# Choosing two of three experts from token 0's own logits, with new orders for the attention stage

## What is computed

```python
x = x + matmul(fake_quant(layernorm(x)), fake_quant(ctx))          # (2,512,1024) @ (2,1024,1024)
h = layernorm(x)
ratio = mean|h[:, 153:]| / (mean|h[:, :153]| + 1e-8)               # one number per batch
logits = concat([h, ratio]) @ gate_w + gate_b                      # 3 logits per token
scores = softmax(logits); top_val, top_idx = top_k(scores, 2)
top_val = top_val / (sum(top_val) + 1e-8)
for i in range(2):
    e = top_idx[:, 0, i]                                           # token 0 chooses for the batch
    x = x + top_val[..., i:i+1] * (act_e(h @ w1[e] + b1[e]) @ w2[e] + b2[e])
```

## Time and profile before

| | us |
|---|---|
| median of 3 runs (406.9, 407.07, 407.93) | 407.07 |
| the profiled execution, whole time | 406.77 |
| its span, first to last instruction | 405.0 |
| TensorE busy | 389.3 |
| VectorE busy | 329.0 |
| ScalarE busy | 196.2 |
| GpSimd busy | 57.9 |

### The profile page before, as it was taken

One profiled execution on the slowest core, in us unless ns is written; L12 is line 12 of the kernel. 1 busy time (PEld: TensorE's weight loads), 2 busy tenths in 40 slices (PEclk: granted clock), 3 DMA queues, 4 the chain that ended last, 5 costly groups with the idle time before them and its releaser, 6 DMA issues.

```text
span 405.0 us, 5336 instructions
## 1 busy us (share of the span) xinstructions
PE 389.3 (96%) x1932; PEld 307.2 (76%) x1932; DVE 329.0 (81%) x512; ACT 196.2 (48%) x254; POOL 57.9 (14%) x78
## 2 busy tenths in 40 slices
PE   2998989999999999999999999999999999999996
PEld 1445736888878888888888888888888888888885
DVE  8699877187999987898799996496998965949983
ACT  3578554174337633671826355342476333425720
POOL 8748400000000002572100004000000000000000
PEclk9999999999999999999999999999999999999999
DMA  8992039523003788000000399600045770000112
GB/s 316 413 407 112 2 108 376 193 84 124 2 0 106 258 252 259 9 0 2 0 0 2 107 368 387 229 2 0 2 146 217 246 256 18 2 0 1 54 52 104
DMA packets 23326, 52.82 MB, mean 130 GB/s; under 512 B 1761, under 2 KB 1793, under 8 KB 23297
## 3 DMA queue, kind: packets, MB, share of 16 engines
q1 hardware_dynamic: 22592, 50.34, 35.0%
q0 software_dynamic: 640, 2.10, 1.5%
q10 hardware_dynamic: 64, 0.02, 0.0%
HBM read 48.26 MB, written 4.19 MB: 130 GB/s over the span
## 4 chain that ended last, share of the span: by engine, by line
PE 94%; DVE 2%; DMA 1%; ACT 1%; issue 1%; ACTq 1%; DVEq 0%
PE ps L1579 43%; PE ps L1551 38%; PE ps L1345 7%; PE ps L1391 2%; PE ps L1377 2%; DMA b1n<-in_L_ffn_b_dram 1%; PE ps L1354 1%; PE ps L1277 1%; ACT q1T L569 1%; PE ps L1412 1%; DVE xres L859 0%; ACTq L666 0%; PE ps L1333 0%; PE ps L1318 0%; ACT hT_hi L593 0%
## 5 line engine op out<-in xcount | busy, mean ns | idle before, releaser
L634 ACT ACTIVATE w_hi<-raw 128x1024 fp32r<-128x1024 f32 x88 | 88.5, 1053 | 45.5 <-DVE raw L985 23.9
L954 DVE TENSOR_TENSOR w_lo<-raw,w_hi 128x1024 fp32r<-128x1024 f32 x88 | 103.4, 1219 | 1.7 <-ACT w_hi L634 1.2
L1579 PE MATMUL ps<-hT_hi,w_hi 128*128 128x512 f32 x256 | 100.0, 390 | 0.0
L1579 PE MATMUL ps<-hT_lo,w_hi 128*128 128x512 f32 x256 | 99.7, 389 | 0.0
L1579 PE MATMUL ps<-hT_hi,w_lo 128*128 128x512 f32 x256 | 99.7, 389 | 0.0
L1551 PE MATMUL ps<-w_hi,a_hi 128*128 128x512 f32 x224 | 87.7, 392 | 0.7 <-DVE a_lo L1027 0.7
L1551 PE MATMUL ps<-w_hi,a_lo 128*128 128x512 f32 x224 | 87.2, 390 | 0.0
L1551 PE MATMUL ps<-w_lo,a_hi 128*128 128x512 f32 x224 | 87.2, 389 | 0.0
L722 ACT ACTIVATE act_f<-ps,b1T 128x512 f32<-128x512 f32 x32 | 22.1, 689 | 104.0 <-PE ps L1579 104.0
L1579 PEld LDWEIGHTS ps<-hT_hi,w_hi 128*128 128x128 f32 x256 | 48.1, 188 | 10.1 <-issue 0.2
L1579 PEld LDWEIGHTS ps<-hT_hi,w_lo 128*128 128x128 f32 x256 | 48.1, 188 | 10.1
(11 more groups left out here) (153 smaller groups left out, 376.2 us busy)
## 6 DMA issues: line engine op xcount, KB each, us to landing
raw<-in_L_ffn_w_dram SPq DMA_DIRECT2D x64, 512.0 KB, 5.5
raw<-in_ctx_dram SPq DMA_DIRECT2D x16, 512.0 KB, 11.5
xres<-in_x_dram SPq DMA_DIRECT2D x8, 512.0 KB, 9.6
b2row<-in_L_ffn_b_dram SPq DMA_DIRECT2D x4, 512.0 KB, 6.6
out_dram<-xres POOLq DMA_DIRECT2D x8, 256.0 KB, 8.0
out_dram<-xres SPq DMA_DIRECT2D x8, 256.0 KB, 2.0
small<-in_L_xattn_x_scale_dram ACTq DMA_DIRECT2D x2, 0.0 KB
small<-in_L_xattn_x_zp_dram ACTq DMA_DIRECT2D x2, 0.0 KB
```

Of the source, the lines that this page charges most:

```text
L634: nc.scalar.activation(w_hi[n % SLOTS][:, 2 * c:2 * c + 2, :], region(q)[:, 2 * c:2 * c + 2, :], ACT.Copy).then_inc(w_hi_ready, 1)
L954: V.tensor_tensor(w_lo[n % SLOTS][:, 2 * c:2 * c + 2, :], region(n % QUARTERS)[:, 2 * c:2 * c + 2, :], w_hi[n % SLOTS][:, 2 * c:2 * c + 2, ...
L1579: last = T.matmul(ps[:, G1_BANK + f % 2, :], w[q % SLOTS][:, k % TT, fs], h[:, k, :], start=n == 0, stop=n == 3 * KT - 1)
```

## The change

**Choosing.** `token_logits(b)` is new: 16 products whose stationary operand is the single column of token 0 of hT_hi or hT_lo and whose moving operand is the 8 columns of gate weights. They give token 0's logits in one partition, before the logits of the other tokens exist. `token_scores` reads them; `choose_experts` adds the router bias and compares the biased logits rather than the exponentials, so it needs neither `gate_turn` nor `gate_exp`. The maximum and minimum over all tokens that it used to leave for `gate_values` move into `gate_values`. `router_bias` is split in two (`ratio_sums`).

**b1.** Its transpose joins `turn_gate_weights` at the start; `turn_bias` on PE and `load_bias` on ACT go; DVE copies it in `gate_weights`.

**Memory and banks.** lgT of batch 0 gets a place of its own; b2row still holds batch 1's, so SP waits for batch 1's `gate_turn` ahead of b2row of pair 2. Q1T_BANK[5] is 4 (was 3), RATIO_BANK[0] is 5 (was 1).

**Orders.** SP loads context tiles 0 and 1 ahead of x tiles 2 and 3. The four tables change, and the lists of all engines with them. Batch 1's `add_terms` 0 to 2 now follow group f = 0 of the first expert, and its last token tile follows f = 1. In pair 0 the `bias_add` calls move from f = 4 to 7 to f = 0 to 3.

```diff
-CTX_ORDER = {"act": [5, 8, 10, 11, 15, 14],
-             "dve": [2, 4],
-             "pool": [0, 1, 3, 6, 7, 9, 12, 13]}
+CTX_ORDER = {"act": [0, 3, 4, 6, 8, 10, 11, 15],
+             "dve": [2],
+             "pool": [1, 5, 7, 9, 12, 13, 14]}
...
+            load_ctx(0)
+            load_ctx(1)
             load_x(2)
             load_x(3)
-            load_ctx(0)
-            load_ctx(1)
...
+                if p == TOP_K:
+                    sp.wait_ge(logit_ps, B)
                 sp.dma_start(b2row[:], b2[bass.ds(e, 1), :].to_broadcast([P, D])).then_inc(b2_in, 16)
...
+            def token_scores(b):
+
+                dve.wait_ge(token_ps, b + 1)
+                V.tensor_copy(token[:, 0:8], ps[0:1, LOGIT_BANK, 0:8]).then_inc(token_read, 1)
+                dve.wait_ge(token_read, b + 1)
+                then(V.tensor_tensor(token[:, 8:8 + NE], token[:, 0:NE], token[:, 4:4 + NE], ALU.add))
...
             def choose_experts(b):
 
-                dve.wait_ge(exp_ready, b + 1)
...
+                dve.wait_ge(token_read, b + 1)
+                then(V.tensor_tensor(token[:, 12:12 + NE], token[:, 8:8 + NE], gbias[0:1, :], ALU.add))
...
             def gate_values(b):
 
                 top, _, mid, a, c, d, e, f = (sel[:, i, :] for i in range(8))
+                dve.wait_ge(exp_ready, b + 1)
+                V.tensor_tensor(a, ex[:, 0, :], ex[:, 1, :], ALU.max)
+                then(V.tensor_tensor(c, ex[:, 0, :], ex[:, 1, :], ALU.min))
+                then(V.tensor_tensor(top, a, ex[:, 2, :], ALU.max))
...
+            def token_logits(b):
+
+                if b:
+                    pe.wait_ge(act_ready, TOP_K * KT)
+                else:
+                    pe.wait_ge(gw_ready, 1)
+                    pe.wait_ge(x1_ready, 3)
+                pe.wait_ge(hT_lo_ready, 2 * b * TT + 2)
+                n = 0
+                for k in range(KT):
+                    for h in (hT_hi, hT_lo):
+                        last = T.matmul(ps[0:1, LOGIT_BANK, 0:8], h[:, k, 0:1], gw_parts[:, k, :],
+                                        start=n == 0, stop=n == 2 * KT - 1)
+                        n += 1
+                last.then_inc(token_ps, 1)
...
-                    if p == 0 and f >= TT:
-                        bias_add(p, k)
-                    if p > 0 and f < TT:
+                    if f < TT:
                         bias_add(p, f)
...
                 if p == 1:
+                    token_scores(1)
                     h_lo(1, 2)
                 t1_sum(p)
+                if p == 1:
+                    ratio_sums(1)
+                    router_bias(1)
+                    choose_experts(1)
                 result(p, 1)
```

More of the change, by code:

```diff
@@ L133, in build @@
         b2row = sb("b2row", [P, D], F32)
-        lgT = b2row[0:8, 0:S]
         ctxq = [sb(f"ctxq{b}", [P, KT, D], F16, act_at + b * (KT * D * 2 + 2 * D * 4)) for b in range(B)]
@@ L153, in build @@
         ident_b = sb("ident_b", [P, P], F16, o); o += P * 2
+        gwn = sb("gwn", [KT, P * NE], F32, o)
+        lgT = [sb("lgT", [8, S], F32, o)[:], b2row[0:8, 0:S]]; o += S * 4
         assert o <= at_weights_end
@@ L595, in split_h @@
                                          ACT.Copy).then_inc(hT_hi_ready, 1)
-            def load_bias():
-                act.wait_ge(b1T_ps, 1)
-                nc.scalar.activation(b1T[:], ps[:, B1T_BANK, 0:NE * KT], ACT.Copy).then_inc(b1T_ready, 1)
             def gate_logits(b):
@@ L606, in gate_logits @@
                     act.wait_ge(logit_ps, b)
-                nc.scalar.activation(lgT, ps[0:8, LOGIT_BANK, :], ACT.Copy).then_inc(logitT_ready, 1)
+                nc.scalar.activation(lgT[b], ps[0:8, LOGIT_BANK, :], ACT.Copy).then_inc(logitT_ready, 1)
             def gate_exp(b):
@@ L909, in choose_experts @@
             def choose_experts(b):
[L911 to L923 removed]
+                dve.wait_ge(token_read, b + 1)
+                then(V.tensor_tensor(token[:, 12:12 + NE], token[:, 8:8 + NE], gbias[0:1, :], ALU.add))
+                score = lambda e: token[0:1, 12 + e:13 + e]
+                one = lambda i: pick[0:1, i:i + 1]
+                large, small_, top, low = (token[0:1, i:i + 1] for i in range(4))
+                V.tensor_tensor(large, score(0), score(1), ALU.max)
+                then(V.tensor_tensor(small_, score(0), score(1), ALU.min))
+                V.tensor_tensor(top, large, score(2), ALU.max)
+                then(V.tensor_tensor(low, small_, score(2), ALU.min))
+                V.tensor_tensor(one(0), score(0), top, ALU.is_lt)
+                V.tensor_tensor(one(1), score(1), top, ALU.is_lt)
+                V.tensor_tensor(one(2), score(1), low, ALU.is_le)
+                then(V.tensor_tensor(one(3), score(2), low, ALU.is_le))
                 V.scalar_tensor_tensor(out=expert[0:1, 2 * b:2 * b + 1], in0=one(1), scalar=1.0, in1=one(0),
@@ L1120, in _ @@
             ctx_constants()
+            x_offset()
             q1_scales(0, 1)
             q1_scales(1, 1)
-            x_offset()
-            term_constants()
             x_stats(2)
+            x_stats(3)
+            load_q1T(1)
             quant_ctx(2)
-            x_stats(3)
-            quant_ctx(4)
-            gate_weights()
             q1_scales(2, 2)
             quant_x(2)
-            load_q1T(3)
+            quant_x(3)
+            term_constants()
+            gate_weights()
             x_stats(4)
             x_stats(5)
+            split_row_term(0)
             split_col_term(0)
-            split_row_term(0)
             q1_scales(4, 2)
@@ L1142, in _ @@
             h_stats(1)
+            h_stats(2)
+            h_lo(0, 0)
             attn_add(0, 3)
-            h_lo(0, 0)
-            h_stats(2)
+            token_scores(0)
             h_stats(3)
@@ L1149, in _ @@
             x_stats(7)
+            tokens_abs(0)
             h_lo(0, 2)
+            ratio_sums(0)
+            router_bias(0)
             q1_scales(6, 2)
-            quant_x(7)
-            tokens_abs(0)
+            choose_experts(0)
             h_lo(0, 3)
             load_q1T(6)
-            router_bias(0)
+            load_q1T(7)
             choose_scores(0)
-            choose_experts(0)
-            gate_values(0)
+            w_lo_chunk(0, 0)
             split_row_term(1)
             split_col_term(1)
-            attn_add(1, 0)
-            attn_add(1, 1)
-            w_lo_chunk(0, 0)
+            gate_values(0)
             w_lo_chunk(0, 1)
@@ L1167, in _ @@
             w_lo_chunk(1, 1)
-            attn_add(1, 2)
+            attn_add(1, 0)
+            attn_add(1, 1)
             for p in range(PAIRS):
@@ L1186, in _ @@
                         else:
-                            pass
+                            attn_add(1, 2)
                     elif f == 1:
@@ L1244, in _ @@
                     choose_scores(1)
-                    choose_experts(1)
                 result(p, 4)
@@ L1409, in gate_turn @@
                 pe.wait_ge(logitT_ready, b + 1)
[L1410 removed]
+                if b:
+                    pe.wait_ge(ratio_read, b + 1)
+                else:
+                    pe.wait_ge(hT_lo_ready, 2 * TT)
                 for t in range(TT):
[L1412 removed]
+                    last = T.matmul(ps[:, TURN_BANK[b], 4 * t:4 * t + 4], lgT[b][:, t * P:(t + 1) * P], pick_logit[:],
                                     start=True, stop=True)
@@ L1481, in _ @@
             transpose_h(0, 0)
-            turn_bias()
-            transpose_q1(4)
             transpose_q1(5)
+            codes_product(1, 0, 0)
+            codes_product(1, 0, 1)
+            codes_product(1, 0, 2)
+            codes_product(1, 0, 3)
+            codes_product(1, 0, 4)
+            codes_product(1, 0, 5)
+            token_logits(0)
+            transpose_h(0, 1)
             codes_product(1, 1, 0)
```

192 lines of the change are left out of this document (87 added, 105 removed).

## The result

The changed kernel takes 410.43 us (median of 17 runs, 407.7 to 411.34); the kernel before, on the same chip, 407.15 us (17 runs, 406.6 to 408.54). The ratio is 1.0061, 95% interval 1.0043 to 1.0079. The forecast was 409.2, slower.

A forecast was written before the change was run, and what follows sets the result against it. The prediction took PE's work plus idle time as the bound. Terms -3.2 -0.7 -0.1 +0.3 +1.4 +4.5 = +2.2 us on the profiled 406.77 gave 409.0, median 409.2; range 406.6 to 411.0, own range 408.3 to 410.1.

The forecast's parts named there:

- token_logits: 16 single-column products on PE in each batch: +0.7 us, twice, with bounds of 0.3 and 0.96.
- (b): Last gate_product waits for hT_lo of tile 3 behind the choice on DVE, which POOL's quant_x holds 0.8: +1.6 us.
- held twice or cold longer: Rival, 410.7 us, chance 0.22: POOL's h_tile also holds token_scores, or half rate at the start lasts 3 us longer.
- (d): In f = 0, PE's second weight chunk waits for w_lo, behind split_col_term and gate_values on DVE: +2.3 us.
- (a): transpose_h of tile 3 waits for hT_lo of tile 2, behind x_stats and tokens_abs on DVE: +0.4 us.
- (c): gate_logits and gate_turn follow the last gate_product with nothing between: +0.2 us.
- The old waits: Five PE waits in the first 65 us (q1T, lgT, scores, split column term, attn_add) all go: -3.2 us.
- The bias move: Pair 0's bias additions leave f = 4 to 7 for 0 to 3, removing PE's wait at late_lo: -0.7 us.
- The start: ACT quantises context tile 0 ahead of x tile 0, so the first q1T comes about 0.5 us later: +0.3 us.

The follow-up runs named there:

- before_tile4: The kernel before with pair 0's bias additions in f = 0 to 3 and x tile 4 turned and loaded ahead of tile 5: 406.68 us.

## Why the prediction was right, and where it wasn't

The direction, the range and the largest term were right; the time was 1.2 us short, and misses of opposite signs stand behind that. So luck has a part in it: token_logits and (b) were put 0.9 too high and the bias gain 0.6 to 1.3 too low, and that made up for a good part of the 1.6 that was missing. The measured 410.43 lies above the forecast's own range, 408.3 to 410.1, and 0.3 from the number of the rival "held twice or cold longer" (410.7). But neither of that rival's two mechanisms is in the trace: token_scores isn't held, and the half rate at the start isn't 3 us longer.

- **The wait for w_lo (d), +2.3 forecast, 2.2 measured.** Right in place, size and cause: gate_values directly ahead, and gone when they were moved.
- **The wait ahead of the fourth gate product (b), +1.6, measured 1.3.** Right in cause. POOL held the choice 0.85 us as forecast 0.8; the dependent chain beside it was 0.5 and not 0.8. The prediction counts the row of 1.69 us as agreeing with the rule on two SBUF inputs; that row is a tensor_scalar with one large input, so only the row of 0.90 is a case of it.
- **(a) and (c), +0.4 and +0.2.** Measured 0.6, and 0.2 at gate_turn with 0.2 more at sum_abs, which had no term. 0.4 too little together.
- **The half rate behind the wait: no term, 1.6 us measured**, in 12 of 17 runs. This is the step that failed. The prediction looked at the clock at the start only and treated a wait as costing what it lasts. Of the 3.8 us that the wait cost, 1.6 were behind it. The rival "cold longer" had the half rate at the start of the kernel, which is another place.
- **token_logits, +0.7 twice, measured 0.40 each.** Mis-sized: I took the value near the row of the 128-column product, and it was near the lower end. The Trainium skill ("TensorE: Matmul & The Clock Gate", Back-to-back issue gap) had 25 ns a product; 0.40 us for 16 agrees.
- **The old waits, -3.2.** All are gone from the trace but the 0.2 at gate_turn, which (c) counts again, and before_tile4 shows that the largest of them, 1.25 us, couldn't be had by itself in the kernel before.
- **The bias move, -0.7, measured 1.3 to 2.0.** Mis-sized, because I read the wait in one trace as the worth of the move. By the chain the stop of 0.7 cost 1.0 already. That VectorE's chain hung on a transfer, and that PE's wait was a remainder (0.7 in one trace, 0.15 in the other), could have been suspected from the pause ahead of w_lo in the groups f = 4 to 5.
- **The start, +0.3.** In the profiled executions +0.9, but the start scatters by as much: first codes products came at 11.78 and 12.37 in two traces of before, at 12.4 to 13.1 in the changed kernel's variants. So the median shift is about 0.5 and not sharper than that.

By the trace-sized terms the change would be: old waits and b1 -3.1, new waits +4.3, token_logits +0.8, start +0.5, bias -1.3 to -2.0, half rate +1.6, which is +2.1 to +2.8 for the runs with the half rate (measured +3.3) and +0.5 to +1.2 for those without (measured +0.75). Within the scatter, the runs at full clock are accounted for; for the others 0.5 to 1.2 us stays open. The two groups are 2.6 us apart, and 3.7 in the variant with the start undone, while the half-rate stretch costs 1.6 in the trace. The start, last section, may hold the rest; no trace of a run of the changed kernel at 1.00 is there to show it.

## What to carry to other kernels

A wait of PE can cost more than it lasts: look at the spacing of the products behind it, compare the whole stretch with one that has no stop, and where a long wait can't be removed, put work into it or split it. Before a VectorE step is moved ahead of another, ask which of the two somebody waits for: gate values that nobody used yet stood ahead of weights that PE was waiting for, and moving one call behind three others was worth 3.8 us, 1.6 of it in the half rate. And a small remainder of a wait in one trace is no measure of its cause: follow it back to the transfer or engine that sets it, since the usual run may hold more of it.

## What the runs showed of the hardware

- The granted clock fell to 0.50 behind a PE wait of 2.2 us, for about 3.4 us, at a place where PE had run at full rate for 45 us with pauses of up to 1.31 us. Behind waits of 0.86, 1.13, 1.31 and 1.50 us (the last in the variant with x tile 4 ahead) it did not, and behind the same 2.2 us it did in 30 of 41 runs of four kernels. What decides among these is open.
- A stop in a row of second-layer products cost 0.3 us more than the idle time in its row: 39.08 us for 168 products with 0.71 idle, 38.51 with 0.15, 38.08 with none.
- At the start the rate changes at a moment that varies from run to run, and the clock column doesn't show it. The same 16 first codes products, in two variants that don't differ before 60 us:

```profile
13.04 4.50 PE L1359 MATMUL ps<-ctxq,q1T 128*128 128x512 f16 x16 [0.44 <-ACT q1T L571]
```

```profile
13.08 5.42 PE L1361 MATMUL ps<-ctxq,q1T 128*128 128x512 f16 x16 [0.45 <-ACT q1T L571]
```

4.50 against 5.42 us, with 1.00 in the clock column for both. It moves everything behind by 0.9 us, which is as much as most edits here are worth, so single traces can't be compared by their span.
